# Elu ahead of shares and masks, kept rows on other queues, no drain behind the branch, and a new split of the mask in the second attention

## What is computed

```python
def _L0_gnn_ref(input, adj, W, a):
    ...
    h = jnp.matmul(input, W)
    ...
    e = jax.nn.leaky_relu(f1[:, :, None] + f2[:, None, :], negative_slope=ALPHA)
    logits = jnp.where(adj > 0, e, NEG_BIG)
    attention = jax.nn.softmax(logits, axis=1)
    h_prime = jnp.matmul(attention, h)
    return jax.nn.elu(h_prime)
...
def _L0_ffn_ref(x, gamma, beta, Wr, br, W1, b1, W2, b2):
    ...
    logits = jnp.einsum('bsd,de->bse', xn, Wr) + br
    top_vals, top_idx = jax.lax.top_k(logits, K)
    w = jax.nn.softmax(top_vals, axis=-1)
    ...
    for e in range(E):
        h = jax.nn.gelu(jnp.einsum('bsd,dh->bsh', xn, W1[e]) + b1[e], approximate=False)
        y_e = jnp.einsum('bsh,hd->bsd', h, W2[e]) + b2[e]
        y = y + y_e * w_full[..., e, None]
    return y
...
def _L1_gnn_ref(hidden, adj, a0, a1, a2, a3):
    ...
    def edge_score(a):
        s = jnp.einsum('bid,bjd->bij', hidden * a, hidden)
        return jax.nn.leaky_relu(s, LEAKY_SLOPE)
    ...
    alpha = jnp.where(adj == 1, e0, NEG_INF)
    ...
    alpha = jax.nn.softmax(alpha, axis=-1)
    return jnp.matmul(alpha, hidden)
...
x = x + _L0_gnn_ref(_layernorm(x, axis=-1), adj, L0_gnn_W, L0_gnn_a)
x = x + _L0_ffn_ref(_layernorm(x, axis=-1), ...)
x = x + _L1_gnn_ref(_layernorm(x, axis=-1), adj, L1_gnn_a0, L1_gnn_a1, L1_gnn_a2, L1_gnn_a3)
x = x + _L1_ffn_ref(_layernorm(x, axis=-1), ...)
return x
```

## Time and profile before

| what | value |
|---|---|
| median of 3 runs | 1109.36 us (1108.39 to 1111.3) |
| the profiled execution | 1109.42 us |
| its span, first to last instruction | 1107.7 us (1.7 lie outside) |
| granted clock of TensorE, mean | 0.987 |
| PE busy | 1024.3 us (92%) |
| DVE, ACT, POOL busy | 754.5, 738.8, 380.1 us |

### The profile page before, as it was taken

How to read it: one execution, slowest core, us unless ns; L and a number is a source line. 1 busy time by engine, 2 the same in 40 slices (tenths; PEclk the granted TensorE clock), 3 DMA queues, 4 the chain that set the end, 5 groups by cost and what they waited for, 6 DMA issues and landing times. The chain is left out here.

```text
span 1107.7 us, 20068 instructions
## 1 busy us (share of the span) xinstructions
PE 1024.3 (92%) x6404; PEld 743.3 (67%) x6445; DVE 754.5 (68%) x2204; ACT 738.8 (67%) x1144; POOL 380.1 (34%) x470
## 2 busy tenths in 40 slices
PE   4898988887997989799999999999999999999995
PEld 4566665554665778488888888885566666666665
DVE  4888898786553365588899989754446666666534
ACT  4888777776653556578888888876655656556550
POOL 4135778887570504456656562110000000000000
PEclk9999999999999999899999999999999999999998
DMA  9978988732276754333323332202015545545101
GB/s 310 351 277 296 400 322 298 246 113 83 71 253 239 200 181 133 103 87 89 88 84 90 91 92 62 59 11 77 1 58 172 170 148 176 171 145 178 39 10 32
DMA packets 81099, 166.29 MB, mean 150 GB/s; under 512 B 11246, under 2 KB 37468, under 8 KB 79964
## 3 DMA queue, kind: packets, MB, share of 16 engines
q1 hardware_dynamic: 72220, 147.10, 39.6%
q0 software_dynamic: 8192, 16.79, 5.0%
q10 hardware_dynamic: 576, 1.05, 0.3%
HBM read 110.24 MB, written 54.66 MB: 149 GB/s over the span
## 5 line engine op out<-in xcount | busy, mean ns | idle before, releaser
L2442 PEld LDWEIGHTS eY<-Vo,dGW 128*128 128x128 f32 x1024 | 132.5, 192 | 54.1 <-issue 52.8
L604 POOL DMA_INDIRECT sorted_x<-V,AT_I x128 | 125.9, 983 | 57.6 <-issue 36.8
L793 PE MATMUL O<-Y,HS 128*128 128x512 f32 x256 | 130.4, 630 | 12.8 <-DVE Vo L1167 12.7
L2442 PE MATMUL eY<-Vo,dGW 128*128 128x128 f32 x1024 | 134.3, 276 | 0.2
L2425 PE MATMUL eU<-XTN,V 128*128 128x512 f32 x256 | 130.9, 594 | 0.8 <-PEq L2329 0.8
L2433 PE MATMUL eU<-H,V 128*128 128x512 f32 x256 | 131.1, 594 | 0.0
L2017 POOL DMA_INDIRECT W<-sorted_y,ROW_I x96 | 96.7, 1008 | 70.2 <-remote 25.3
L2525 ACT ACTIVATE H<-eU,bn 128x512 f32<-128x512 f32 x128 | 99.5, 777 | 25.5 <-PE eU L2425 16.2
L2118 PEld LDWEIGHTS f_O<-f_XN,f_PT 128*128 128x128 f32 x896 | 106.8, 192 | 12.7 <-DVE X L2229 10.4
L2118 PE MATMUL f_O<-f_XN,f_PT 128*128 128x128 f32 x896 | 109.8, 276 | 3.8 <-DVE X L2229 2.2
L2622 DVE TENSOR_TENSOR dGW<-H,WBC 128x512 f32<-128x512 f32 x80 | 55.2, 692 | 82.5 <-PE eY L2442 82.3
(11 more groups left out here) (331 smaller groups left out, 2056.1 us busy)
## 6 DMA issues: line engine op xcount, KB each, us to landing
XTN<-in_adj SPq DMA_DIRECT2D x64, 512.0 KB, 7.5
entries<-in_adj SPq DMA_DIRECT2D x64, 512.0 KB, 3.5
masks<-NMW SPq DMA_DIRECT2D x8, 2048.0 KB
f_MK<-masks SPq DMA_DIRECT2D x60, 256.0 KB, 2.8
sorted_y<-zero SPq DMA_DIRECT2D x36, 256.0 KB
NMW<-sorted_x SPq DMA_DIRECT2D x25, 256.0 KB
sorted_y<-NMW SPq DMA_DIRECT2D x25, 256.0 KB, 2.6
X<-in_x SPq DMA_DIRECT2D x8, 512.0 KB, 9.0
```

The lines of the kernel that those rows point to most:

```text
L604: g_.indirect_dma_start(sorted_x, bass.IndirectOffsetOnAxis(ap=AT_I[b % 2][:, kt:kt + 1], axis=0), XR[b % 2][:, t * P:(t + 1) * P], None). ...
L793: pe.matmul(O[:, h * HALF:(h + 1) * HALF], HS[:, g % 3, :], Y[:, g % 4, h * HALF:(h + 1) * HALF], start=False, stop=(c == NT - 1)).then_in ...
L2442: i = pe.matmul(Y[q][:, t * P:(t + 1) * P], GW[:, j % 2, t * P:(t + 1) * P], Vo[:, e * P:(e + 1) * P], start=(e == 0 and t == 0), stop=(e ...
```

## The change

- **First attention.** BY_VECTOR goes from 4 to 3: DVE makes the tiles 0, 1 and 2, ACT 3 to 7, two of these at c = 0 of a batch and the others at c = 4, 5 and 6. DVE's `elu` stands right behind the share of c = 2, ahead of the mask of that step and of the next shift; `shares` moves to c = 3. PE's turn of the last but one batch gets a wait on the table.
- **Kept rows.** Batches 1 to 5 of `kept_x` are stored by SP right behind the last masks, before the blocks; 6 and 7 by ACT at blocks 16 and 18; 0 by ACT at block 33.
- **Gathers.** The gathers of tiles 6 and 7 of batch 1 (four transfers) move from the end of the expert blocks to the start of GpSimd's program in the second attention, with a semaphore of their own.
- **Second attention.** LOWER = 256: PE's mask matmul covers 256 columns instead of 512, DVE's subtract 768 instead of 512.
- **End.** The last stage's block drains GpSimd at its end, and the block of the branch that is taken doesn't.

```diff
-BY_VECTOR = 4
+BY_VECTOR = 3
...
                 keep(LAST)
                 sp.wait_ge(kept, 16 * B)
+                for b in range(1, LAST - 1):
+                    for h in range(2):
+                        sp.wait_ge(x_added[h], b + 1)
+                    sp.dma_start(kept_x[b, :, :], X[:, b * N:(b + 1) * N]).then_inc(kept, 16)
...
-                    if RING < k < RING + B:
-                        keep_x(k - RING)
                 for k in range(NB - 6, NB):
                     store(k)
-                sp.wait_ge(x0_done, X0_MEANS)
-                keep_x(0)
                 sp.wait_ge(kept, 16 * 2 * B)
...
-                    gather(1, t)
+                    if t < NT - 2:
+                        gather(1, t)
...
+                    if b == LAST - 1 and h == 0:
+                        pe.wait_ge(table_step, TAKEN)
...
-                    if c == 3 and b >= 1:
-                        grown(b - 1)
                     relu(g)
...
+                    if c == 2 and b >= 1:
+                        grown(b - 1)
                     if c == 3 and b < LAST:
                         copy_h(b + 1, 2)
-                    if BY_VECTOR <= c < NT and b < LAST:
-                        convert(b + 1, c)
+                    if b < LAST:
+                        for t in (((), (), (), (3,), (4,), (5,), (6, 7), ()) if b == 0 else ((3, 4), (), (), (), (5,), (6,), (7,), ()))[c]:
+                            convert(b + 1, t)
...
+                    if k in (RING + E, RING + E + 2):
+                        keep_x(LAST - 1 + (k - RING - E) // 2)
+                    if k == JOIN + NT + 1:
+                        act.wait_ge(x0_done, X0_MEANS)
+                        keep_x(0)
...
-                    if c == 3 and b >= 1:
-                        elu(b - 1)
                     shift(g)
                     if g >= 1:
                         share(g - 1)
+                    if c == 2 and b >= 1:
+                        elu(b - 1)
...
-                    if c == 2 and b >= 2:
+                    if c == 3 and b >= 2:
                         shares(b - 2)
...
-                        for t in (((), (), (), (0, 1), (2, 3), (), (), ()) if b == 0 else ((0, 1), (), (2, 3), (), (), (), (), ()))[c]:
+                        for t in (((), (), (), (0, 1), (2,), (), (), ()) if b == 0 else ((0, 1), (), (2,), (), (), (), (), ()))[c]:
...
-            RING = 4
+            RING, LOWER = 4, HALF // 2
...
+                for t in range(NT - 2, NT):
+                    gather1(t)
...
-                        return pe.matmul(T[g % 2][:, 0:HALF], minusb[:, :], mask(g)[:, 0:HALF], start=False, stop=True,
-                                         skip_group_check=(g, 0) in raw_at)
+                        return pe.matmul(T[g % 2][:, 0:LOWER], minusb[:, :], mask(g)[:, 0:LOWER], start=False, stop=True,
+                                         skip_group_check=True)
...
-                    v.tensor_tensor(R4[:, g % 2, HALF:N], R4[:, g % 2, HALF:N], mask(g)[:, HALF:N], ALU.subtract).then_inc(barred, 1)
+                    v.tensor_tensor(R4[:, g % 2, LOWER:N], R4[:, g % 2, LOWER:N], mask(g)[:, LOWER:N], ALU.subtract).then_inc(barred, 1)
...
-            block = ctx.enter_context(nc.Block(no_gpsimd_drain=search))
+            block = ctx.enter_context(nc.Block())
...
         with nc.Else():
             with ExitStack() as ctx:
-                block = ctx.enter_context(nc.Block())
+                block = ctx.enter_context(nc.Block(no_gpsimd_drain=True))
```

More of the change, by code:

```diff
@@ L501, in store @@
                                  YB[:, k % RING, 0:tiles_of(k), :]).then_inc(yb_stored[k % 2], 16)
-                def keep_x(b):
-                    for h in range(2):
-                        sp.wait_ge(x_added[h], b + 1)
-                    sp.dma_start(kept_x[b, :, :], X[:, b * N:(b + 1) * N]).then_inc(kept, 16)
                 def late(n):
@@ L1037, in tail_row, with keep_x @@
                                         zero[:, :].rearrange("p (t d) -> p t d", d=P)).then_inc(tail_rows, 16)
+                def keep_x(b):
+                    for h in range(2):
+                        act.wait_ge(x_added[h], b + 1)
+                    nc.scalar.dma_start(kept_x[b, :, :], X[:, b * N:(b + 1) * N]).then_inc(kept, 16)
                 def copy_bx(k):
@@ L2019, in gather, with gather1 @@
                                                          ).then_inc(gathered[t // 2], 16)
+                def gather1(t):
+                    for k in range(2):
+                        at_ = 2 * NT + k * NT + t
+                        nc.gpsimd.indirect_dma_start(y1[:, k * NT + t, :], None, sorted_y,
+                                                     bass.IndirectOffsetOnAxis(ap=ROW_I[:, at_:at_ + 1], axis=0)
+                                                     ).then_inc(rest_gathered, 16)
                 def root(b):
@@ L2079, in half @@
                             i = pe.matmul(T[g % 2][:, lo * P:(h + 1) * HALF], xta(b)[:, r * P:(r + 1) * P],
-                                          xt(b)[:, lo * P:(h + 1) * HALF], start=first, stop=(h == 1 or (g, 0) in raw_at))
+                                          xt(b)[:, lo * P:(h + 1) * HALF], start=first, stop=True)
                             if (g, h) in raw_at:
@@ L2692, in _ @@
                 def _(pool):
-                    by_software = [shared_sems[f"gathered{k}"] for k in range(4)]
+                    by_software = [shared_sems["rest_gathered"], *(shared_sems[f"gathered{k}"] for k in range(4))]
                     for s in (*shared_sems.values(), *last_sems.values()):
```

12 lines of the change are left out of this document (7 added, 5 removed).

## The result

The changed kernel takes 1100.56 us (median of 3 runs, 1098.81 to 1102.3), against 1109.36 before: a ratio of 0.9917, with a 95% interval of 0.9892 to 0.9943. That is faster by 8.8 us, and inside the range. The profiled execution is the fastest of the three, 1098.81 us with a span of 1097.0, so its stages are compared with those of before by their spans (10.7 us apart), and 1.8 us of that difference is luck of that one execution.

A forecast was written before the change was run, and what follows sets the result against it. TensorE's own work bounds the second attention and last stage, with its waits elsewhere and GpSimd's sends ending the first attention. Sum: 1109.4 - 4.0 - 6.9 - 3.3 - 1.0 + 3.4 = 1097.6 us, range 1088 to 1103.

The forecast's parts named there:

- Branch end, -4.0: End of program: without GpSimd's drain in the branch, the end follows TensorE's drain, 4.0 us earlier.
- Rival C: End of program: the drain moves but its price stays, since the end drains GpSimd anyway; 1101.6 us, chance 0.08.
- Expert blocks, -6.9: Expert blocks: with kept_x stores off SP's block loads, five TensorE waits for block rows vanish, 6.9 us saved.
- Rival B: Expert blocks: only SP's issue time returns as transfers still crowd block loads; -3.9 instead of -6.9, 1100.6 us, chance 0.12.
- Boundary, -3.3: Blocks to second attention: SP spared kept_x(0)'s issue and most of its wait, four gathers moved; stage starts 3.3 us earlier.
- First attention, -1.0: First attention: earlier elu shortens batches 1 to 3 before GpSimd's sends, less a loss at the start; net 1 us saved.
- its 1.7 us: First attention: a shorter wait after batches 3 and 5 may avoid the drop to 1.2 GHz, returning 1.7 us each time.
- Second attention, +3.4: Second attention: TensorE's mask matmul saves 6.8 us, but VectorE's longer subtract raises TensorE's waits from 2.5 to 12.7; net +3.4.
- The stepping: Second attention: both engines stepped through 64 steps with trace durations and three edges; 279.95 us with old numbers, 283.4 with new.
- What I said would show it: Second attention: stage 3 to 4 us longer, TensorE's waits for added rows near 10 us, VectorE's idle under 1 per batch.
- Rival A: Second attention: VectorE's addition is hidden and the stage stays TensorE's; -5.4 instead of +3.4, 1088.8 us, chance 0.20.
- Rival D: First attention: ScalarE's two masks at each batch's head lengthen seven batches, 15.8 us in all; slower, 1114.4 us, chance 0.03.

The follow-up runs named there:

- d1: The kernel before with only GpSimd's drain moved, to the end of the last stage's block: 1105.90 us, ratio 0.9969.
- k1: Changed kernel with the kept_x stores of batches 1 to 7 issued by ScalarE at blocks 9 to 15, the eighth left at block 33: 1104.38 us.
- u2: Changed kernel with the first attention as before (masks, elu, shares and exp at their old places): 1098.02 us.
- u3: Changed kernel with both attentions as before, leaving the kept rows on other queues, the moved gathers and the drain: 1092.82 us.
- s2: Changed kernel with TensorE's mask matmul back at 512 columns and VectorE's subtract left at 768: 1099.78 us.
- u1: Changed kernel with the second attention's mask split back at column 512 (TensorE 512, VectorE 512): 1093.58 us.
- c1: Changed kernel with the old second-attention split and four masks on VectorE again; only the new order of elu, exp and shares stays: 1086.87 us.
- u4: Changed kernel with all kept_x stores back on SP, seven in blocks 9 to 15, the eighth at the blocks' end: 1109.90 us.

## Why the prediction was right, and where it was not

The forecast was 1097.6 us in a range of 1088 to 1103; 1100.56 lies inside, and the way (faster) was right. The gain was 8.8 of the 11.8 forecast. That the sum came so near is in part luck: in the profiled execution the first attention was 2.45 us worse than forecast and the blocks 2.35 better, which cancel; the second attention was 1.4 worse, and the median lies 1.8 above that execution. Step by step:

- **Branch end, -4.0.** Right: -4.06 in the trace, and TensorE's branch is the next limit as said. Alone it is 3.3 us by medians (4.5 in the trace of d1). Rival C is out.
- **Expert blocks, -6.9.** The mechanism was right; the profiled pair shows -9.25, the means of the kernels -7.4. The term left out that a wait of TensorE costs 0.22 us more than its idle time, 1.1 in all. The argument for it misread one pair of steps: 6.76 us with a store of kept rows against 3.78 with a weight load don't compare, since the first also writes zeros to `sorted_x`, with a register load of its own. The same step without kept rows takes 5.15 in the changed kernel, so the store of kept rows stretched it by 1.6 and not by 3:

```profile
322.02 0.36 SPq L496 DMA_DIRECT2D NMW<-sorted_x  x1
...
327.17 0.36 SPq L496 DMA_DIRECT2D NMW<-sorted_x  x1
```

Rival B, that only SP's issue time of 3.9 us comes back, is out for the part as a whole. For the issues alone it is not far off: k1 takes nothing but them off SP and gains 4.6 (by the finishes) to 5.5 us. What B had wrong is that the transfers would still crowd this stretch; most of them left it, and that gave the other 3.4 to 3.7. B was the Trainium skill's rule ("DMA: Bandwidth & Descriptors", "Issuing engines are not separate DMA queues"), by which starting transfers from several engines saves only the time to start them. In its other half, that transfers share the same engines whoever starts them, k1 fits it: with ScalarE starting them, 3.4 to 3.7 us of the gain were lost.

- **Boundary, -3.3.** Right: -3.66. Of the clock I counted nothing and kept 2 us for the range. The changed kernel is at a granted 0.75 over the first 6.9 us of the second attention, where it was at 0.51 in the earlier trace rows; by the stages above (old split, 297.1 against 296.6 in the mean) that was worth some 0.5 us, and a clock at 2.4 GHz throughout (u2) goes with 1.7 more:

```profile
439.50:446.40 6.90, 5.75 (x12) 2.22 (x12) 2.19 (x3) 2.87 (x5) 4.79 (x6) 0.75 0.67 208
```

- **First attention, -1.0.** Wrong in sign: +1.45 in the profiled execution and +1.1 by the means of the first turns, though not clear of noise as said above. The step that failed is that ScalarE's two masks only delay the exp by 1.3 and that the batch makes it up. The delay landed on the copies of the transposed rows, for which TensorE then waited 15.3 us, and in batch 3 the masks stand waiting for a tile that lands at 113 us. The trace of before showed both: ScalarE's copies right behind the second step's relu, and the tiles' landings; I priced neither. Nor did the clock give its 1.7 us back: the changed kernel has three stretches at 1.2 GHz ahead of the blocks (at 119, 201 and 215 us), as many as before (122, 187 and 214). And I did not see that the order alone, without the masks, is worth 4.4 us in this stage and 6.4 in all; I had the 1.9 us per batch as what VectorE would allow, and then let ScalarE's masks eat it.
- **Second attention, +3.4.** The mechanism was right: the longer subtract delays the adds, the attend waits, and the stage is longer than before. The size was +4.8, 1.4 more, and the shorter stretch at low clock hides some of it: at like clock it is 5.2 to 5.5. The batches 3 to 5 take 37.2 us each where they take 36.3 with the old split (u3). The stepping left out edges such as TensorE's wait for VectorE's statistics; that these make up the miss is not shown:

```profile
PE f_M L2080 <- DVE b L237: 1.0, 5, 0.3
```

What I said would show it was partly wrong: TensorE's waits for the adds are 6.0 us and not near 10. More of it stands with the weight loads, which wait for the same adds (PEld in the second attention, before and changed):

```profile
PEld f_O L2118 <- DVE X L2229: 11.6, 26, 1.1
```

```profile
PEld f_O L2136 <- DVE X L2247: 20.2, 35, 1.8
```

Rival A (hidden, -5.4) is out by s2. Rival D had the right place, ScalarE's masks at the head of a batch, and more than twice the price: with the order kept new, the masks' move costs 6.7 us (u1's 1093.58 against c1's 1086.87, on different chips, of which 4.6 lie in the first attention of the traces) and not 15.8. It did not make the kernel slower, since the new order of elu pays for most of it.

## What to carry to other kernels

Take a change apart that touches several stages, and measure each part: here three parts brought 16.5 us, two took 8 back, and one of these two held a reorder worth 6.4 us next to a move of work that cost as much. Look at the spread of a stage between kernels that share its program before you explain a microsecond of one pair of traces. Before moving work onto an engine that has idle time in the sum, look at what stands behind it in that engine's row and when its own data lands. A queue that issues in a tight loop is a resource: a store that nothing waits for still costs when it stands ahead of loads that are waited for.

## What the runs showed of the hardware

In k1's longest step, with kept rows (512 KB a transfer) under way, three of SP's register loads took 0.74 to 0.91 us against 0.26 to 0.39, though ScalarE had started the transfers, and the step from load to load 6.2 us against 4.8. A wait of TensorE for a block's rows cost 0.22 us more than its idle time, in all five waits of the kernel before and all five of u4. GpSimd's drain took 7.9 us after some 340 us in which it had nothing to do, and 9.95 right behind its last work. Kernels with 3.4 us at TensorE's lower clock at the head of the second attention took 1.7 to 1.9 us longer over the stage than those with none.
